# A fused attention, mixture-of-experts and recurrence kernel: the routing product of the dense chunks moves from VectorE to GpSimd

## The reference

```python
x = x + _L0_attn_ref(xn, ...) + _L0_ffn_ref(xn, ...)      # linear attention; 16 experts, 6 per token
xn = _layernorm(x, axis=-1)
x = x + _L1_attn_ref(xn, ...) + _L1_ffn_ref(xn, ...)      # tanh recurrence; 8 experts, 2 per token, and a shared one
...
for e in range(E):                                        # _L0_ffn_ref, experts of 176 units
    g = h @ w_gate[e].T
    u = h @ w_up[e].T
    out = jax.nn.silu(g) * u @ w_down[e].T
    y = y + cw[:, e:e + 1].astype(x.dtype) * out
...
def step(state, u_t):                                     # _L1_attn_ref
    s = jnp.tanh(u_t + state * gamma + beta)
    return (s, s)
```

## Time and profile before

| | |
|---|---|
| median of 3 executions | 701.4 us (700.51 to 704.57) |
| the profiled execution's own time | 703.51 us |
| its span, first to last instruction | 701.8 us |
| TensorE busy | 632.3 us, 90% |
| VectorE busy | 485.5 us, 69% |
| ScalarE busy | 368.8 us, 53% |
| GpSimd busy | 254.3 us, 36% |
| mean granted TensorE clock | 0.97 |

### The profile page before, as it was taken

The page is one execution under the profiler, slowest core; times in us unless marked ns, Lnnn a source line. Parts: engine busy times, 40 slices in busy tenths (PEclk is TensorE's granted clock), DMA queues, the critical chain, the costliest instruction groups (busy, mean ns, idle before and its releaser), DMA issues.

```text
span 701.8 us, 12651 instructions
## 1 busy us (share of the span) xinstructions
PE 632.3 (90%) x3607; PEld 344.4 (49%) x3607; DVE 485.5 (69%) x1515; ACT 368.8 (53%) x1008; POOL 254.3 (36%) x267
## 2 busy tenths in 40 slices
PE   6999999999899988989999978999868899888976
PEld 2664444544444433444544433454454577566644
DVE  7965775667835777875787876667783656774685
ACT  3445455456446456467556555645456647563450
POOL 5246222222241235332134423123511352662582
PEclk8999999999999999999999999999997999999997
DMA  8105478753675238545445520507222254851132
GB/s 303 50 1 182 158 253 258 247 178 102 217 287 177 92 120 244 186 141 172 158 154 181 191 90 1 206 11 118 68 54 61 78 150 124 175 152 65 53 106 83
DMA packets 91228, 99.06 MB, mean 141 GB/s; under 512 B 30478, under 2 KB 81774, under 8 KB 90734
## 3 DMA queue, kind: packets, MB, share of 16 engines
q10 hardware_dynamic: 45840, 46.40, 20.3%
q1 hardware_dynamic: 39950, 37.21, 18.1%
q0 software_dynamic: 5376, 14.69, 7.0%
HBM read 27.96 MB, written 64.03 MB: 131 GB/s over the span
## 4 chain that ended last, share of the span: by engine, by line
PE 34%; DVE 21%; issue 17%; ACT 13%; POOL 6%; DMA 3%; POOLq 1%; ACTq 0%; DVEq 0%
PE Y L704 10%; DVE zbuf L1707 8%; PE G L704 6%; PE U L704 5%; ACT RING L1278 5%; PE U L1024 3%; PE Y L811 3%; POOL hl L1848 2%; PE Y L1059 2%; POOL W L1898 2%; ACT scr L1237 2%; ACT hh L1248 2%; DVE scr L1724 2%; DVE scr L1719 1%; DMA yrows<-scr 1%
## 5 line engine op out<-in xcount | busy, mean ns | idle before, releaser
L1848 POOL TENSOR_TENSOR hl<-scr,hh 128x512 f16<-128x512 f32 (+2 forms) x100 | 117.6, 1176 | 305.3 <-ACT hh L1248 303.8
L1707 DVE TENSOR_TENSOR_SCAN zbuf<-gam,RING 128x32 f32<-128x32 f32 x512 | 155.6, 304 | 90.8 <-ACT RING L1278 89.8
L1278 ACT ACTIVATE RING<-zbuf 128x16 f32<-128x16 f32 x512 | 111.0, 217 | 178.3 <-DVE zbuf L1707 172.6
L704 PE MATMUL G<-xT,W 128*128 128x512 f16 (+2 forms) x600 | 148.1, 384 | 10.6 <-ACT scr L1237 5.8
L704 PE MATMUL U<-xT,W 128*128 128x512 f16 (+2 forms) x600 | 147.7, 383 | 0.0
L704 PE MATMUL Y<-hh,W 128*128 128x512 f16 x352 | 119.7, 381 | 17.7 <-POOL hl L1848 17.4
L704 PEld LDWEIGHTS G<-xT,W 128*128 128x128 f16 (+3 forms) x600 | 59.9, 103 | 78.2 <-issue 13.1
L1719 DVE TENSOR_TENSOR scr<-scr,U 128x512 f32<-128x512 f32 (+2 forms) x100 | 67.4, 674 | 43.9 <-PE U L704 30.3
L704 PEld LDWEIGHTS U<-xT,W 128*128 128x128 f16 (+3 forms) x600 | 61.9, 103 | 69.7 <-issue 2.3
L1237 ACT ACTIVATE scr<-G 128x512 f32<-128x512 f32 (+2 forms) x100 | 58.7, 587 | 43.0 <-PE G L704 42.8
L1248 ACT ACTIVATE hh<-scr 128x512 f16<-128x512 f32 (+2 forms) x100 | 61.8, 618 | 31.8 <-DVE scr L1724 24.6
(11 more groups left out here) (198 smaller groups left out, 833.6 us busy)
## 6 DMA issues: line engine op xcount, KB each, us to landing
xrows<-zeros ACTq DMA_DIRECT2D x15, 1280.0 KB, 5.8
yrows<-zeros ACTq DMA_DIRECT2D x12, 1536.0 KB, 6.0
stage<-weights SPq DMA_DIRECT2D x20, 384.0 KB
yrows<-scr POOLq DMA_DIRECT2D x48, 128.0 KB
yrows<-zeros ACTq DMA_DIRECT2D x3, 1408.0 KB, 5.6
stage<-weights SPq DMA_DIRECT2D x14, 256.0 KB
parked<-RING SPq DMA_DIRECT2D x1, 3520.0 KB, 12.7
W<-parked SPq DMA_DIRECT2D x1, 3520.0 KB, 11.3
```

The lines of the kernel that those rows point to most:

```text
L704: last = nc.tensor.matmul(bank_, w(wp), act(ap), start=start and n == 0, stop=stop and n == count - 1)
L1278: nc.scalar.activation(RING[:, (t + 1) % RING_T, ::2], zbuf[:, 1::2], ACT.Tanh).then_inc(state_done, 1)
L1707: nc.vector.tensor_tensor_scan(zbuf[:, :], gam[:, :], RING[:, t % RING_T, :], 0.0, ALU.mult, ALU.add)\
L1848: nc.gpsimd.tensor_tensor(hl[rows, a, :], h32[a][rows, :], hh[rows, a, :], ALU.subtract)\
```

## The change

The weight is multiplied onto `sg`, in place, by GpSimd (`weigh`), before VectorE's gated product rather than after it. VectorE's `routed` is gone, `gated` waits for `weigh` where it waited for `silu`, and `h_head` waits for `gated`. Where `h_done` guarded the reuse of the `CS` buffers, the new semaphore `weighed` does.

```diff
@@ spread, on ScalarE
-                    act.wait_ge(h_done, (phase - 1) * CH0)
+                    act.wait_ge(weighed, (phase - 1) * CH0)
@@ h_head, on ScalarE
-                    act.wait_ge(h_done, n + 1)
+                    act.wait_ge(gated_done, n + 1)
@@ gated, on VectorE
-                dve.wait_ge(silu_done, dense + 1)
+                if isinstance(n, int) and n >= DENSE0:
+                    dve.wait_ge(silu_done, dense + 1)
+                else:
+                    dve.wait_ge(weighed, n + 1)
                 dve.wait_ge(up_done, dense + 1)
...
-            def routed(phase, n, a):
-                dve.wait_ge(gated_done, n + 1)
-                dve.wait_ge(spread_copied, phase + 1)
-                nc.vector.tensor_tensor(h32[a], h32[a], spread_slot(phase), ALU.mult).then_inc(h_done, 1)
@@ the pair, on VectorE
                         step_and(HALF * a)
-                        if a or not isinstance(k, int) or k:
-                            routed(phase, n + a - 1, 1 - a)
-                        elif phase:
-                            routed(phase - 1, n - 1, 1)
                         for i in range(1, HALF - 1):
                             step_and(HALF * a + i)
                         gated(n + a, a)
@@ on GpSimd
+            def weigh(phase, n, a):
+
+                pool.wait_ge(silu_done, n + 1)
+                pool.wait_ge(spread_copied, phase + 1)
+                nc.gpsimd.tensor_tensor(sg[a], sg[a], spread_slot(phase), ALU.mult).then_inc(weighed, 1)
...
                 def pair(k, tick, pieces, late, woven):
                     n = phase * CH0 + 2 * k
+                    weigh(phase, n, 0)
                     if phase or not isinstance(k, int) or k:
                         h_tail(n - 1, 1)
+                    weigh(phase, n + 1, 1)
                     h_tail(n, 0)
```

More of the change, by code:

```diff
@@ L260, in build @@
         gated_done = sem("gated_done")
-        h_done = sem("h_done")
+        weighed = sem("weighed")
         hhead_done = sem("hhead_done")
@@ L644, in load_tiles @@
                 if r == RING_XG // 2:
-                    sp.wait_ge(h_done, DENSE0)
+                    sp.wait_ge(weighed, DENSE0)
                 if r >= RING_XG:
@@ L1775, in _ @@
                 unit_step(0)
-                if u == 0:
-                    routed(BLOCKS - 1, n - 1, 1)
                 if kind(n - 2) == "R":
```

## The result

The changed kernel takes 754.97 us (median of 6 executions, 750.42 to 758.53 and one of 1292.09 that is left out of the comparison), against 702.1 us before (6 executions, 700.51 to 706.3). The ratio is 1.0732, with a 95% interval of 1.07 to 1.0765: slower by about 50 us. The profiled execution spans 748.8 us where the one before spans 701.8, so 47.0 us are to be found in the traces; the medians are 52.9 us apart, since the profiled execution was the fastest of the six (750.42).

The account below looks back on a forecast made before the run. The recurrence of scans and tanhs from 222 to 493 us was taken as the bound, TensorE close behind. 42.6 - 10.6 - 5 + 2 + 4 + 1 gave +34 us on 703.5, stated as 737 us, range 715 to 760.

Parts of the forecast that it names:

- slow product: Rival: each weigh takes 1.44 us, with the indirect transfers' upper bound 755 us; chance 0.14, shared with the falling clock.
- falling clock: Rival: longer TensorE idles lower its granted clock, adding up to 20 us, 765; chance 0.14, shared with the slow product.
- Lock of the weigh: In the 52 chunks with steps each weigh holds one scan, 0.82 us each: +42.6 us, bound from below 33.
- Duration: In the 52 chunks with steps the weigh takes 1.20 us instead of the tail's 1.156: +2 us, from above +15.
- Removed product: In the chunks with steps, where woven work fills VectorE, `routed` leaves the chain: -10.6 us.
- Crossings of TensorE: Where the chain runs through TensorE's products, 6 weighs lie beside it and cost nothing: -5 us, -16 if all crossed.
- Scatter: At 9 pairs two indirect transfers hold GpSimd ahead of the weigh, +0.5 us each: +4 us, bounds 0 and 9.
- 163 to 222 us: About four weighs meet VectorE's sorting of weights, and `routed` leaves the chain there: +1 us.
- Before and after: First stretch: TensorE is the bound and the weigh is covered, zero; the second layer's units are not touched.
- the weigh doesn't hold the scans: Rival, chunks with steps: the weigh is short or comes between scans, so no lock; 691 us, chance 0.04.
- TensorE takes most of it: Rival: weighs in chunks with front work are absorbed by TensorE; about +9 us, 712 us, chance 0.16.

Follow-up runs that it names:

- e1: The kernel before with the routed product left out on every engine, so the experts' outputs stay unweighted; 687.46 us, ratio 0.9761 to before.
- e3: The changed kernel with the weigh over 256 of its 512 columns; 716.33 us, ratio 1.0196 to before.
- e6: The kernel before with the float16 tails of the 52 chunks with steps moved from GpSimd to VectorE; 693.61 us, ratio 0.9862 to before.
- e8: e6 with the tails of the second layer's shared expert, but for the last two, on VectorE too; 687.2 us, ratio 0.9764 to the kernel before.

## Why the prediction was right, and where its sizes were off

The mechanism was right, and so were the sign and the place: two long scans of six per plain chunk, the opening one at 1.08 under the tail and the third under the weigh, TensorE's share below 85%, the stretch before 163 us unchanged (160.7 for 161.3), the gated product not waiting in plain chunks. The measured 755 lies in the range, 18 us above the forecast. That it lies in the range is in part luck. The forecast's own band was +22 to +46 us; the spans are 47.0 us apart and the medians 52.9. The room above that band was made for a slow product and a falling clock, and neither came. The smaller signs were a little low too: opening scans 5.1 to 5.2 us apart (5.24 measured), a mean scan of 0.46 (0.518), a weigh of at most 1.25 (1.267).

On the spans, +47.0 us stand against the sum of +34:

- **Lock of the weigh**, +42.6, with the duration's +2, the scatter's +4 and the crossings' -5: 43.6. Measured as changed kernel against e1: 53.7. This is the term that was mis-sized. The hold was worked out as 0.82 us and 0.04 for the duration; it is 1.06, and 52 x 0.20 is 10.4 us. It has two parts, the due time and the duration. The working took the third scan's due time from the profile before, 0.18 us behind the weigh's start, but the removal of `routed` moves just that scan forward. Without `routed` the second tanh starts 1.71 us behind the opening scan (412.36) and not 1.85 (390.49 - 388.64), because it starts 0.10 us before the silu's recorded end. So the third scan is due 0.06 us into the weigh and not 0.18, and is held for nearly all of it.
- **Duration**, 1.20 us taken, 1.267 measured. The two-input rows were the nearest, as chosen, but the weigh takes 0.11 us more than the tail, a subtraction with a float16 input and a float16 result. Which of these differences costs it, no run parts. The estimate from the Trainium skill's GPSIMD Engine Reference, 1.11 us, is further off; here the measurement decides.
- **Removed product**, -10.6: e1 gives -8.4 in the stretch. And the two terms don't add as written. In a plain chunk the removal buys 0.13 us (4.33 to 4.20), but the third scan's end is then set by the weigh's end, which hangs on the silu. The chunk's +0.93 is 1.06 - 0.13, so the earlier due time gains 0.13 and is charged 0.13 more hold.
- **Crossings of TensorE**, -5: about right. Against e1, the eight chunks that grew by less than a hold fall 4.4 us short of it together. 2.6 us of these are in chunks 36, 58 and 82, where TensorE's lines lead the chain of e1. For the other five, among them chunks with woven VectorE work, what covers the hold is not shown.
- **Scatter**, +4: right in sum, about 3.5 us. The first chunks of six of the nine pairs grew by 0.47 to 0.63 us more than plain ones, the other three did not. In four of the six `gated` starts 0.03 us behind the weigh's end, the wait that the working named.
- **163 to 222 us**, +1: measured +4.1, with the wait for `parked` 4.7 us longer, a transfer that the working didn't look at.
- **Before and after**: nothing predicted, -0.6 and -1.8 measured. That e1 gains 5.4 us before chunk 23 shows that `routed` wasn't free there, as "TensorE is the bound" had it. The first heads wait for it: ScalarE's queue in the kernel before, at the very first chunks,

```profile
63.05 0.63 ACT L1248 ACTIVATE hh<-scr 128x512 f16<-128x512 f32 x1 [2.55 <-DVE scr L1724]
...
69.70 0.63 ACT L1248 ACTIVATE hh<-scr 128x512 f16<-128x512 f32 x1 [4.07 <-DVE scr L1724]
```

The changed kernel got only 0.6 of these 5.4 us: in 18 of its first 24 chunks `gated` starts within 0.12 us of the weigh's end, so it waits for the weigh there instead. With the half weigh (e3) 3.0 us come.

Of the 13 us between 34 and 47, 10.1 are the lock with its crossings and scatter, 2.2 the smaller removal, 3.1 the stretch 163 to 222, and -2.4 the ends.

The rivals: that the weigh doesn't hold the scans fell with the rows above. That TensorE takes most of it fell as well, since it took some 4 us of 55. e6 shows that it was the next bound in the other direction, for a kernel made faster. The slow product with an upper-bound scatter, 755 us, comes near the time but by a product of 1.44 us, which it isn't; the granted clock of the execution, 0.973, is that of before.

## What to carry to other kernels

When a chain of short VectorE instructions with two SBUF inputs sets the time, each GpSimd product, tail or copy that a link meets costs the chain what is left of that instruction's duration, whatever it computes, unless another engine sets the pace at that place; busy shares hide this, because a held instruction counts as busy, so compare its maximum and mean with its median. Costing a move to GpSimd needs the due time of the next such instruction in the changed order, not in the old one, since an edit that removes work ahead of it moves it into the lock. Where GpSimd can't be avoided, cut its instruction at the length of the gap between two links; better, put the product on VectorE in the idle time that the chain leaves, as e6 and e8 did (1.4% and 2.4% faster than the kernel before).

## What the runs showed of the hardware

- GpSimd, 128 partitions: 512 columns float32 times float32 into float32 1.267 us (median), the tail into float16 1.156, 256 columns of the product 0.743, a copy with one input 0.611. So 256 more columns of the product cost 0.52 us.
- A GpSimd instruction with one SBUF input holds a VectorE scan as one with two does (0.61 us for 0.22).
- Between two GpSimd products that stand back to back, 1.41 us in all, a waiting VectorE scan gets in.
- A TensorE idle of 3.85 us (e6) was followed by a down product and then by a gate product of 2.77 us; in the earlier trace rows it is 2.64 us. The granted clock of that product's stretch is 0.50, the lower of its two levels (0.53 in the stretch of the 2.64 us product); the timeline, then the window:

```profile
402.49 0.39 PE L705 MATMUL Y<-hh,W 128*128 128x512 f16 x1 [3.85 <-DVE hl L1730]
...
404.04 2.77 PE L705 MATMUL G<-xT,W 128*128 128x512 f16 x6
```

```profile
404.04:406.81 2.77, 2.77 (x8) 1.06 (x7) 2.24 (x7) 1.37 (x5) 0.00 (x0) 0.50 0.00 0
```
